# A linear-attention block with a quantised FFN: a new order of the opening, and the FFN weight made in tiles 1 to 3

## The reference

```
h   = layernorm(x)
q, k, v = split(h @ W_attn + b_attn)          # W_attn 512 x 1536, 16 heads of 32
q, k = elu(q) + 1, elu(k) + 1
for each token t, each head:                  # causal linear attention
    kv += k_t (outer) v_t ;  ksum += k_t
    y_t = (q_t @ kv) / (q_t . ksum + 1e-6)
x1  = x + y @ W_proj + b_proj
h2  = layernorm(x1)
out = x1 + fp8(h2) @ fp8(W_ffn).T + b_ffn     # fp8 e4m3, clipped to +-448
```

## Time and profile before

| | us |
|---|---|
| median of 3 runs | 950.37 |
| the profiled execution, whole | 948.85 |
| its span, first to last instruction | 947.1 |
| PE busy | 918.2 (97%) |
| DVE busy | 731.8 (77%) |
| ACT busy | 745.6 (79%) |
| POOL busy | 641.3 (68%) |
| share of PE in the chain that ended last | 90% |

### The profile page before, as it was taken

One profiled execution on the slowest core, in us unless ns is written; L12 is line 12 of the kernel. 1 busy time (PEld: TensorE's weight loads), 2 busy tenths in 40 slices (PEclk: granted clock), 3 DMA queues, 4 the chain that ended last, 5 costly groups with the idle time before them and its releaser, 6 DMA issues.

```text
span 947.1 us, 44776 instructions
## 1 busy us (share of the span) xinstructions
PE 918.2 (97%) x19470; PEld 490.5 (52%) x19532; DVE 731.8 (77%) x1404; ACT 745.6 (79%) x1358; POOL 641.3 (68%) x713
## 2 busy tenths in 40 slices
PE   5998999999999999999999999999999999999896
PEld 2455555555555555555555555555555555555454
DVE  6999879787777777778687687777778687676687
ACT  5788787877869688787877868788787878868874
POOL 5659877766767677676776667677676676764433
PEclk9999999999999999999999999999999999999999
DMA  8926564565464554565555465555555455462421
GB/s 268 143 41 109 109 119 103 97 119 97 95 122 100 98 116 104 96 114 105 95 114 107 91 116 106 89 118 108 92 114 112 89 114 110 90 103 59 76 69 59
DMA packets 252036, 99.12 MB, mean 105 GB/s; under 512 B 232384, under 2 KB 232640, under 8 KB 251840
## 3 DMA queue, kind: packets, MB, share of 16 engines
q1 hardware_dynamic: 251840, 96.25, 52.3%
HBM read 22.81 MB, written 16.78 MB: 42 GB/s over the span
## 4 chain that ended last, share of the span: by engine, by line
PE 90%; POOL 3%; issue 2%; ACT 2%; DVE 2%; SPq 1%; DMA 1%; ACTq 0%; POOLq 0%
PE R L235 77%; PE S L235 13%; POOL st L1029 1%; POOL xn L1031 1%; DMA x2t<-x2b 0%; ACT raw L477 0%; POOL xs L1076 0%; PE R L239 0%; DVE raw L739 0%; POOL raw L1062 0%; DMA xs<-in_L_attn_x 0%; ACT ktok L477 0%; SPq L1227 0%; DVE v L728 0%; ACT o L477 0%
## 5 line engine op out<-in xcount | busy, mean ns | idle before, releaser
L235 PE MATMUL R<-xt,wh 128*128 128x512 f16 x1024 | 306.2, 381 | 2.4 <-ACT wh L477 2.4
L716 DVE SCALAR_TENSOR_TENSOR qk<-qk,rel 128x512 f32<-128x512 f32 x128 | 112.8, 884 | 118.1 <-ACT rel L489 118.1
L477 ACT ACTIVATE raw<-qk 64x512 f32<-64x512 f32 x256 | 160.8, 628 | 48.9 <-PE S L235 45.7
L235 PE MATMUL R<-xt,wl 128*128 128x512 f16 x512 | 194.0, 380 | 0.0
L1083 POOL TENSOR_TENSOR yhl<-y,yhl 128x512 f16<-128x512 f32 x60 | 70.0, 1167 | 146.1 <-ACT yhl L477 146.1
L235 PE MATMUL R<-wh,xt 128*128 128x512 f16 x512 | 158.0, 379 | 0.0
L235 PEld LDWEIGHTS R<-xt,wh 128*128 128x128 f16 x1024 | 96.7, 98 | 116.0 <-DVE xt L882 2.6
L739 DVE TENSOR_TENSOR raw<-S,causal 64x1024 f32<-64x1024 f32 x128 | 155.9, 1218 | 0.9
L1029 POOL TENSOR_TENSOR st<-st,half 128x1 f32<-128x1 f32 x127 | 92.7, 730 | 90.6 <-DVE st L705 89.8
L235 PE MATMUL R<-wph,yt 128*128 128x512 f16 (+1 forms) x520 | 132.4, 377 | 3.9 <-ACT yt L477 1.9
L486 ACT ACTIVATE qk<-R,bqk,wm 128x512 f32<-128x512 f32 x128 | 98.9, 773 | 35.6 <-PE R L235 35.0
(11 more groups left out here) (108 smaller groups left out, 1364.8 us busy)
## 6 DMA issues: line engine op xcount, KB each, us to landing
xs<-in_L_attn_x SPq DMA_DIRECT2D x64, 256.0 KB, 3.1
out<-xs SPq DMA_DIRECT2D x63, 256.0 KB, 2.4
raw<-in_L_attn_W_attn SPq DMA_DIRECT2D x3, 1024.0 KB, 9.5
xs<-in_L_attn_W_proj SPq DMA_DIRECT2D x4, 256.0 KB
raw<-in_L_ffn_weight SPq DMA_DIRECT2D x1, 1024.0 KB, 17.0
raw<-raw SPq DMA_TRANSPOSE x63, 3.7
x2t<-x2b SPq DMA_TRANSPOSE x62, 2.5
xt<-xnhl SPq DMA_TRANSPOSE x60, 3.5
```

The costliest lines, as they stand in the source:

```text
L235: return e.matmul(out, a, b, start=start, stop=stop, skip_group_check=True)
L477: return e.activation(out, in_, ACT.Copy, **more)
L716: e.scalar_tensor_tensor(qk[j % 2][:, i, :], qk[j % 2][:, i, :], 1.0, rel[:, (u - 1) % 2, :], ALU.min, ALU.add).then_inc(s_phi, 1)
```

## The change

On the opening:

- The attention weight is loaded in four pieces (`PIECES`: 256, 256, 512 and 512 columns) in place of three of 512, each with a scale of its own. ACT and DVE convert it in eight parts (`PARTS`: four of 128 columns, four of 256) in place of six of 256.
- `attn_size(0)` moves ahead of the third transposed tile on ACT, `scale(0)` on DVE ahead of `t1_parts(2)`, and `most(0)` on PE ahead of `t1(3)`. `most(1)` moves into the first column block, behind its eighth matmul, `most(2)` behind column block 1 and v's `most(3)` behind column block 4.
- PE transposes the identity matrix into an unused PSUM region before, between and behind the transposes of h (`warm`: 16, 3 and 4 times).
- ACT makes the f16 projection weight after the first `phi` of tile 0. DVE makes its low part (`proj_weight`) in tile 1 in place of tile 0, and reads the last `phi` of tile 0 after `update(1)`. `v_scale` stands before the last `phi` of block 0 in place of before the sixth.

On the FFN weight: `ffn_high` moves from DVE's tile 0 to tile 1, `ffn_round` to tile 2, the four sums from DVE's tile 1 to POOL's tile 2 (`ffn_sum` on `s_wfs`), and the four transposes from SP's tile 1 to the end of SP's tile 3. PE, ACT and DVE do no `ffn` in tile 2, and `ffn(0)` and `ffn(1)` in tile 3. The stores of tiles 0 to 2 are issued together in tile 4; the load of tile 14 moves from tile 4 to tile 5.

On POOL: in tiles 1 to 7 `add_bp(n)` alone is left of two; the biases of tiles 8 to 23 are added two by two in tiles 8 to 15.

The core of the diff:

```diff
 # tensor
-            for m in range(4):
-                t1(m)
-            most(0)
+            warm(16)
+            t1(0)
+            t1(1)
+            warm(3)
+            t1(2)
+            most(0)
+            t1(3)
+            warm(4)
             for i in range(12):
                 proj_qkv(0, i)
-                if i in (0, 2, 11):
-                    most((0, 2, 11).index(i) + 1)
+                if i in (1, 4, 11):
+                    most((1, 4, 11).index(i) + 2)
...
-                elif 2 <= n < NT - 1:
+                elif n == 3:
+                    ffn(0)
+                    ffn(1)
+                elif 4 <= n < NT - 1:
                     ffn(n - 2)
 # vector, opening
+            scale(0)
             t1_parts(2)
-            scale(0)
             t1_parts(3)
             attn_weight(0)
             attn_weight(1)
-            v_peak()
             scale(1)
-            ln1(4)
-            attn_weight(2)
-            phi(0, 0)
-            attn_weight(3)
+            attn_weight(2)
+            attn_weight(3)
+            scale(2)
+            phi(0, 0)
+            ln1(4)
+            attn_weight(4)
...
 # vector, tiles
+                    if n == 1:
+                        ahead(chunks(0)[1])
                     if not tail(n):
                         scores(n)
+                    if n == 1:
+                        proj_weight()
                     if n + 8 < NT:
                         ln1(n + 8)
-                    if n == 0:
-                        proj_weight()
                     if n == 1:
-                        ffn_sum(0, 2)
+                        ffn_high()
+                    if n == 2:
+                        ffn_round()
...
-                    if n == 0:
-                        ffn_high()
-                        ffn_round()
-                        ahead(chunks(n)[1])
 # gpsimd
+            def ffn_sum(f):
+                pool.wait_ge(s_wfd, 3)
+                e.tensor_tensor(w_b[:, f, :], w_hi[:, f, :], w_lo[:, f, :], ALU.add).then_inc(s_wfs, 1)
...
+                    elif n < 8:
+                        add_bp(n)
+                    elif n < 16:
+                        add_bp(2 * n - 8)
+                        add_bp(2 * n - 7)
                     elif n + 8 < NT:
                         add_bp(n + 8)
...
+                    if n == 2:
+                        ffn_sum(0)
+                        ffn_sum(1)
                     if n:
                         values(n)
-                    if 1 <= n < 8:
-                        add_bp(n)
...
                     add_bf(n - 1)
+                if n == 2:
+                    ffn_sum(2)
+                    ffn_sum(3)
 # sync
             def t_wf(f):
-                sp.wait_ge(s_wfd, 4 + f)
+                sp.wait_ge(s_wfs, f + 1)
...
-                if n == 1:
-                    t_wf(0)
-                    t_wf(1)
...
-                    t_wf(2)
-                    t_wf(3)
-                if n + 10 < NT:
+                if n == 3:
+                    for f in range(4):
+                        t_wf(f)
+                if n == 5:
+                    load_x(n + 9)
+                if n != 4 and n + 10 < NT:
                     load_x(n + 10)
```

More of the change, by code:

```diff
@@ L141, in build @@
         Y = S[:, :, 4 * HALF:4 * HALF + 4 * W]
-        UN = [wm[:, 7 * i + 4:7 * i + 5] for i in range(4)]
-        UP = [wm[:, 7 * i + 5:7 * i + 6] for i in range(4)]
-        UN_V, UN_P = wm[:, 33:34], wm[:, 34:35]
+        UN = [wm[:, 7 * i + 4:7 * i + 5] for i in range(5)]
+        UP = [wm[:, 7 * i + 5:7 * i + 6] for i in range(5)]
+        UN_V, UN_P = wm[:, 41:42], wm[:, 42:43]
         raw_p = xs[:, NX - 4:NX, :]
@@ L162, in build @@
         s_out = [sem(f"xo{i}") for i in range(NX)]
-        s_wa = [sem(f"wa{i}") for i in range(3)]
+        s_wa = [sem(f"wa{i}") for i in range(4)]
         s_wf, s_wp, s_bqk, s_bva, s_bias = sem("wf"), sem("wp"), sem("bqk"), sem("bva"), sem("bias")
@@ L187, in build, with weights @@
         s_rs1, s_xn, s_rs2, s_x2, s_xb, s_x1b = sem("rs1"), sem("xn"), sem("rs2"), sem("x2"), sem("xb"), sem("x1b")
-        s_yl, s_blank, s_one, s_khl, s_near = sem("yl"), sem("blank"), sem("one"), sem("khl"), sem("near")
+        s_wfs, s_yl, s_blank, s_one, s_khl, s_near = sem("wfs"), sem("yl"), sem("blank"), sem("one"), sem("khl"), sem("near")
         bank = {}
+        def weights(first, end):
+            third, at = divmod(first, D)
+            return raw[:, third, :, at:at + end - first]
         def four(t):
@@ L291, in proj_qkv @@
                     if i == j == 0 and m == 8:
+                        most(1)
                         pe.wait_ge(s_wl, 1)
@@ L500, in proj_size @@
                 act.wait_ge(s_wp, 64)
[L501 removed]
+                e.activation(wpl[:, :, :].bitcast(BF16), raw_p, ACT.Abs, accum_out=wm[:, 28:29]).then_inc(s_size, 1)
             def attn_weight(i):
[L504 to L507 removed]
+                piece = piece_of(PARTS[i][0])
+                act.wait_ge(s_up, piece + 1)
+                copy(wh[:, :, slice(*PARTS[i])], weights(*PARTS[i]), scale=UP[piece]).then_inc(s_wh, 1)
             def proj_weight():
[L510 to L511 removed]
+                act.wait_ge(s_up, 5)
+                copy(wph[:, :, :], raw_p, scale=UP[4]).then_inc(s_wph, 1)
             def ffn_half():
[L515 removed]
+                act.wait_ge(s_wl, part_of(7) + 1)
                 act.wait_ge(s_wfc, 4)
@@ L628, in _ @@
             t1(1)
+            attn_size(0)
             t1(2)
-            attn_size(0)
             t1(3)
@@ L634, in _ @@
             attn_size(1)
-            phi(0, 0)
+            attn_size(2)
             attn_weight(2)
             attn_weight(3)
+            phi(0, 0)
+            attn_weight(4)
             phi(0, 1)
+            attn_weight(5)
             ln1_parts(4)
@@ L659, in _ @@
                         spread(n)
-                        proj_weight()
                     if n >= 2 and not tail(n):
                         t2(n - 2)
-                    ahead(chunks(n)[0])
+                    if n == 0:
+                        ahead(chunks(n)[0][:1])
+                        proj_weight()
+                        ahead(chunks(n)[0][1:])
+                        k_tokens(n + 1)
+                        ahead(chunks(n)[1])
+                        values(n)
+                        queries(n + 1)
+                        ln1_parts(n + 8)
+                    else:
+                        ahead(chunks(n)[0])
                     if tail(n - 1):
@@ L687, in _ @@
                     spread(n + 1)
-                if 2 <= n <= NT and not (n < NT - 1 and tail(n)):
+                if n == 3:
+                    ffn(0)
+                    ffn(1)
+                elif 4 <= n <= NT and not (n < NT - 1 and tail(n)):
                     ffn(n - 2)
@@ L933, in ffn_round @@
                                 saturate=False).then_inc(s_wfd, 1)
-            def ffn_sum(first, end):
-                dve.wait_ge(s_wfd, 3)
-                for f in range(first, end):
-                    e.tensor_tensor(w_b[:, f, :], w_hi[:, f, :], w_lo[:, f, :], ALU.add).then_inc(s_wfd, 1)
             e.memset(pair[:, :], 0.0).then_inc(s_pair, 1)
@@ L953, in _ @@
             attn_weight(1)
-            v_peak()
             scale(1)
+            attn_weight(2)
+            attn_weight(3)
+            scale(2)
+            phi(0, 0)
             ln1(4)
-            attn_weight(2)
-            phi(0, 0)
-            attn_weight(3)
+            attn_weight(4)
             ln1(5)
             phi(0, 1)
-            scale(2)
+            v_peak()
+            attn_weight(5)
             phi(0, 2)
+            scale(3)
+            phi(0, 3)
             ln1(6)
-            attn_weight(4)
-            phi(0, 3)
+            attn_weight(6)
+            phi(0, 4)
+            attn_weight(7)
             ln1(7)
-            attn_weight(5)
-            phi(0, 4)
-            v_scale()
             phi(0, 5)
             phi(0, 6)
+            v_scale()
             phi(0, 7)
@@ L1012, in _ @@
                         scores(n + 1)
-                if n == 1:
-                    ffn_sum(2, 4)
                 if n == NT:
@@ L1185, in _ @@
                 if n == 0:
-                    add_bp(n + 8)
                     add_bp(n)
```

116 lines of the change are left out of this document (54 added, 62 removed).

## The result

| | before | after |
|---|---|---|
| median of the runs of one comparison | 950.86 us (949.42 to 951.57, 4 runs) | 955.79 us (954.99 to 955.86, 4 runs) |
| profiled execution, its span | 948.85, 947.1 us | 954.99, 953.2 us |

The ratio is 1.0048 [1.0032 to 1.0064]: the change costs 4.9 us by the medians, 6.1 by the two profiled spans. The forecast was 957.5, in a range from 952.5 to 963.0.

A forecast was written before the change was run, and what follows sets the result against it. PE was taken as the bound, busy 918.2 of 947.1 us. The terms 0 - 2.1 + 7.1 + 2.1 gave +7.1 us, 955.95 for the profiled execution and 957.5 us for the median, range 952.5 to 963.

The forecast's parts named there:

- opening: Up to k_tokens: PE starts 2.5 us sooner but waits 2.6 us for DVE's phi; 0, bounds +0.8 and -2.5.
- tiles 1 and 2: PE's waits for y at scores(2) and for x2 go, leaving 0.3 us residual; together -2.1 us.
- wait in tile 3: PE's ffn(0) waits for the weight's transposes from S + 12.8 to S + 19.8; +7.1 us, from 6.0 to 10.5.
- clock behind it: After PE's tile 3 wait TensorE falls to its lower clock level; +2.1 us, bounds 0 and 4.2.
- S: Start of PE's scores(3), 92.47 us before the change; tile 3's times are counted from it.
- so I find it free for the sums at S + 4.5: POOL in tile 3 can start the two FFN weight sums at S + 4.5, 1.2 us each, ending at S + 6.9.
- the ramp of the opening: At the opening, 4.2 us of dense PE work at the low clock cost 2.1 us; same cost assumed behind tile 3's wait.
- The first rival: Opening: warming holds, PE works at 2.4 GHz from 13.6 us, DVE less held up; -2.0 more, 955.5 us; chance 0.22.
- I take no gain: Opening: the warming transposes were taken not to raise the clock before 13.6 us; otherwise the opening wins about 2 us.
- the second rival: Tile 1's wait returns longer, DVE 1.5 to 2 us late when stretched beside POOL; 958.5 to 959.5 us; chance 0.13.
- POOL in tiles 8 to 23: One extra add_bp in each of tiles 8 to 15 fits POOL's idle time; 0 to 0.5 us, taken as 0.
- the missing x2t wait: Tile 2: PE's 1.2 us wait for transposed x2 disappears because no ffn runs there.

The follow-up runs named there:

- transposes in the pause: Changed kernel plus 56 identity transposes on PE ahead of ffn(0) in tile 3; 955.55 us, ratio to before 1.0052.
- the weight on time: Changed kernel with FFN and projection weights made in tile 0, sums on DVE and the weight's transposes ahead of t1(11); 947.08 us, ratio to before 0.9962.
- the warmed kernel of before: Kernel before with 23 identity transposes (16, 3, 4) added on PE in its old opening; 950.79 us, ratio to before 0.9995.
- as many instructions: Changed kernel with the opening's 23 identity transposes moved into PE's pause ahead of ffn(0) in tile 3; 960.72 us, ratio to before 1.0099.
- the lighter DVE: New opening with the loops of before, v's scale taken from 128 of 2048 weight elements per partition; 946.74 us, ratio to before 0.9956.

## Why the prediction was right, point by point

The side, the place and the main mechanism, a wait for the weight's transposes in SP's queue, were right; the opening's was not. The terms, in the trace's own time (two traces of one kernel differ by up to 1.1 us in the first tiles):

| term | forecast | measured | from |
|---|---|---|---|
| opening | 0 | -1.9 | start of `scores(0)`, `scores(1)` |
| tiles 1 and 2 | -2.1 | -1.1 | -2.96 at S, less the opening |
| wait in tile 3 | +7.1 | +8.6 | PE's wait |
| clock behind it | +2.1 | +1.1 to +1.25 | granted clock; transposes in the pause |
| sum | +7.1 | +6.7 at tile 4, +6.1 at the end | starts of `scores(n)`, spans |

- *The wait in tile 3* was too small by 1.5 us. The step that failed is "so I find it free for the sums at S + 4.5". POOL started the second pair of sums at 94.48, S + 5.84. The working counts only this pair; the first stands in no term. It runs from 88.06 to 90.20, and the low part of `values(2)` starts behind it at S + 1.5, where before it started at S + 0.3 (92.74), as soon as ACT's part was there. The second layernorm of token tile 1, whose statistics DVE had ready at 90.0, starts at 91.28, and from there POOL is never idle until the FFN bias (L1130) ends at 94.5. So the first pair accounts for 1.2 of the 1.3 us. A sum took 1.07 us, under my 1.2. From there all runs as worked out: the low part ends at S + 11.7 (10.8 forecast), the last transpose starts at S + 18.4 (17.3), lands 2.5 later, and 0.5 more pass until PE's matmul starts, which no term held.
- *The page's rule on two-operand sums* (the Trainium skill, GPSIMD Engine Reference, 4.1 Engine selection) is not borne out here: 1.07 us for a sum on POOL, DVE's was 0.9.
- *The clock* fell as forecast, but most of its low stretch lay in the pause. I had taken the ramp of the opening, where PE works all through, as the price. Of the low stretch of 6.7 us only 2.2 hold matmuls.
- *The opening.* The first rival came true ("the warming holds", 0.22). What I gave against it, the low pitch behind 16 transposes before, had the excuse of their pauses, which I had named and then not followed. With it `most(1)` is sooner and DVE's last `phi` stands at 41.68, not at 45; `k_tokens` comes at 42.91, with a wait of 1.73 (2.6 forecast). Without warming my two times held to 0.1 us (13.50 and 45.07 for 13.6 and 45.0), though PE's wait there was 1.7 in place of 2.6. So the step that failed is "I take no gain": the condition was wrong, the working behind it nearly right.
- *Tiles 1 and 2.* Both waits of 1.2 us went. The wait of tile 1 came back all the same, by another engine than the second rival had it, and at `values(1)`. DVE and then POOL in tile 1, after:

```profile
64.31 2.35 DVE L948 SCALAR_TENSOR_TENSOR wpl<-xs,wm,wph 128x2048 f16<-128x2048 f32 x1
...
67.65 2.28 DVE L960 SCALAR_TENSOR_TENSOR raw<-raw 128x2048 fp8e4<-128x2048 fp8e4 x1
```

```profile
65.01 2.67 POOL L1100 TENSOR_TENSOR xnhl<-xn,xnhl 128x512 f16<-128x512 f32 x1 [0.95 <-ACT xnhl L499]
67.64 2.77 POOL L1083 TENSOR_TENSOR v<-mid,pair 64x264 f32<-64x264 f32 x1
```

  POOL's spread of v takes 2.77 us beside the FFN weight's high part on DVE, 0.63 when that is elsewhere (the weight on time). PE waits 1.45 for it. I had counted DVE's time in tile 1 and called POOL's slack enough.
- *POOL in tiles 8 to 23*: no wait of PE from 125 to 880 us is longer than before's; the difference goes from 6.73 at tile 8 to 6.69 at tile 23. The 0 holds.
- *The medians* differ by 4.9, the spans by 6.1. All four terms were off: by -1.9 in the opening, +1.0 in tiles 1 and 2, +1.5 in the wait and about -0.9 in the clock. They nearly cancel, which is why the time was close; that is luck. For the medians I had put the changed kernel's 1.5 us above its trace; it lay 0.8 above, and the kernel before 2.0.
- *The signs.* Of those named beforehand, the missing x2t wait, the place of the wait and the low level behind it came out. The first projection at 13.6 and a pitch of 0.43 did not (12.95 and 0.216), the wait was over the 6 to 8 us named (8.6), and the profile calls it "issue", not wft.
- *Slips.* The upper bound of the wait adds up to 11.3, not 10.5 (7.1 + 0.8 for t_k, 2.2 for the landing, 1.2 for the sums). The low end of the range takes 6.5 for the wait where its lower bound is 6.0. And PE does pause ahead of tile 60 before, by 1.86 us in `values(59)`; the waits were read only to 130 us. None of it changes the side.

## What to carry to other kernels

When work is moved to a later tile, follow the queue that feeds its consumer instruction by instruction (here POOL, then SP): the written order there cost 8.6 us of wait, and moving four lines of it gave 7. Test a change of several parts one part at a time: this one held an opening worth 5 us by the medians (2.3 by the traces) and a rearrangement of the loops that turned it into a loss. An engine with slack over a tile can still be late at one instruction, if a neighbour stretches just that one.

## What the runs showed of the hardware that was not expected

- Transposes of an f32 identity raise TensorE's clock and hold it: eight f16 matmuls took 1.89 us behind 23 of them and 3.49 without; seven took 1.67 behind 56 in a pause and 2.79 without. It does not last through every wait: in the warmed kernel of before PE waited 1.93 us behind them, and the eight took 3.57.
- The granted clock can fall in or behind a pause of PE of 1.55 to 2.77 us (1.55 with the weight on time, 1.86 without warming, 2.77 with as many instructions), and does not always: it stayed at 1.00 behind the 1.86 us of the kernel before and the 1.55 of the changed one. A low stretch of 3.2 us full of matmuls costs 1.6.
- A POOL operation beside a DVE one of 128x2048 with 16 or 8 bit results took 2.77 us in place of 0.63, and 2.67 in place of 1.16; they ended 0.5 and 1.0 us behind DVE's. Before, a 128x1 subtraction on POOL (0.55 elsewhere) took 2.59 beside the same projection step of DVE in tile 0, and ended 0.4 behind it. The spread is 0.63 when DVE's operation is elsewhere; why POOL's is stretched, no run here shows.
- PE has pauses of 0.3 to 2.1 us which no engine releases. The place of the longest in the tail goes with the number of instructions ahead of it in PE's program, whatever the time: behind the 103rd matmul of `values(59)` in both traces of before, behind the 100th without warming, which has one `most` more, and behind the 62nd matmul of `scores(62)` in six traces with the 23 transposes in the opening; with 23 in tile 3 and one wait instruction more, behind the 61st. Others, like the 1.4 in `values(1)` with the lighter DVE, came up in one trace only. What causes them was not found, and several gains of about 1 us vanished in them or in low stretches of the clock in the tail.
